# A mixture-of-experts layer behind an attention stage: where the routed stage is placed among the chunks of the shared expert, 38 ahead and 26 behind for 40 and 24

## The reference

```python
sg = xf @ shared_gate_w.T
su = xf @ shared_up_w.T
shared_out = jax.nn.silu(sg) * su @ shared_down_w.T      # 1024 hidden
topk_idx, w, _scores = _route(xf, router_w, correction_bias)   # 4 of 16 experts
...
h = jax.nn.silu(g) * u                                   # 128 hidden per expert
hw = h * combine.T[:, :, None]
routed = jnp.einsum('esh,ehc->sc', hw, down_w)
return (shared_out + routed).reshape(B, T, C)
```

## Time and profile before

| | us |
|---|---|
| median of 3 runs | 1007.53 (1004.88 to 1009.16) |
| profiled execution | 1004.85 |
| its span, first to last instruction | 1003.0 |
| granted TensorE clock, share of full | 0.999 |
| PE busy in the span | 985.6 (98%) |
| DVE, POOL, ACT busy | 660.1, 437.1, 380.6 |

### The profile page before, as it was taken

The page is one execution under the profiler, slowest core; times in us unless marked ns, Lnnn a source line. Parts: engine busy times, 40 slices in busy tenths (PEclk is TensorE's granted clock), DMA queues, the critical chain, the costliest instruction groups (busy, mean ns, idle before and its releaser), DMA issues.

```text
span 1003.0 us, 21036 instructions
## 1 busy us (share of the span) xinstructions
PE 985.6 (98%) x6750; PEld 601.2 (60%) x6750; DVE 660.1 (66%) x1534; ACT 380.6 (38%) x776; POOL 437.1 (44%) x508
## 2 busy tenths in 40 slices
PE   9999999999999999999999999999999999999997
PEld 7776744444444444446787777878778744344442
DVE  4977688874588898875455554555545436676767
ACT  3646454433544333223444444444444411111111
POOL 0726422131145222134545444454454167776774
PEclk9999999999999999999999999999999999999999
DMA  9736858878463611416999999999888578988776
GB/s 347 259 121 206 293 182 233 227 206 237 156 179 99 200 62 63 144 35 178 265 269 256 271 267 256 255 269 249 243 242 252 173 210 267 309 272 283 242 239 219
DMA packets 176636, 219.02 MB, mean 218 GB/s; under 512 B 101225, under 2 KB 112361, under 8 KB 175529
## 3 DMA queue, kind: packets, MB, share of 16 engines
q1 hardware_dynamic: 152792, 139.05, 46.6%
q0 software_dynamic: 23760, 78.79, 26.0%
HBM read 124.72 MB, written 70.27 MB: 194 GB/s over the span
## 4 chain that ended last, share of the span: by engine, by line
PE 87%; DVE 5%; issue 3%; DMA 2%; ACT 2%; another core or an unknown queue 0%; POOL 0%; DVEq 0%; SPq 0%; ACTq 0%; POOLq 0%
PE bank L1074 19%; PE bank L948 18%; PE bank L1137 11%; PE bank L964 9%; PE bank L1098 9%; PE bank L1149 5%; PE bank L1057 5%; PE bank L723 2%; PE bank L703 2%; PE bank L1088 2%; PE bank L800 1%; DMA arena<-in_dn_w 1%; PE bank L980 1%; PE bank L713 1%; PE bank L807 1%
## 5 line engine op out<-in xcount | busy, mean ns | idle before, releaser
L948 PE MATMUL bank<-arena 128*128 128x512 f16 x960 | 218.1, 379 | 0.2 <-ACT arena L1330 0.2
L1074 PE MATMUL bank<-arena 128*128 x1716 | 211.2, 273 | 1.0 <-DVE arena L1615 0.8
L1074 PEld LDWEIGHTS bank<-arena 128*128 128x128 f16 x1716 | 162.9, 98 | 26.9 <-issue 2.0
L2070 POOL DMA_INDIRECT arena<-xr_dram,arena x143 | 140.7, 984 | 57.7 <-issue 45.9
L2127 POOL DMA_INDIRECT arena<-y_dram,arena x128 | 134.4, 1050 | 70.9 <-issue 32.9
L948 PEld LDWEIGHTS bank<-arena 128*128 128x128 f16 x960 | 94.2, 99 | 108.2 <-ACT arena L1330 0.7
L1137 PE MATMUL bank<-arena 128*128 128x512 f16 x576 | 129.2, 379 | 1.6 <-issue 1.5
L1098 PE MATMUL bank<-arena 128*128 x429 | 115.4, 378 | 0.5 <-ACT arena L1408 0.5
L1345 ACT ACTIVATE arena<-arena 128x512 f16<-128x512 f32 x64 | 40.3, 629 | 197.8 <-DVE arena L1623 96.0
L1890 DVE SCALAR_TENSOR_TENSOR arena<-bank,arena 128x128 f32<-128x128 f32 x143 | 41.6, 291 | 107.6 <-ACT arena L1397 82.8
L1953 DVE SCALAR_TENSOR_TENSOR arena<-arena 128x512 f32<-128x512 f32 x128 | 95.1, 750 | 25.4 <-DMA arena<-y_dram,arena 16.9
(11 more groups left out here) (226 smaller groups left out, 1281.7 us busy)
## 6 DMA issues: line engine op xcount, KB each, us to landing
y_dram<-arena SPq DMA_DIRECT2D x143, 256.0 KB
arena<-in_x SPq DMA_DIRECT2D x8, 1024.0 KB, 12.4
xr_dram<-arena SPq DMA_DIRECT2D x16, 512.0 KB, 3.8
x_dram<-arena SPq DMA_DIRECT2D x8, 1024.0 KB, 5.6
arena<-in_gu_w SPq DMA_DIRECT2D x16, 512.0 KB, 3.6
out<-arena SPq DMA_DIRECT2D x32, 256.0 KB
arena<-x_dram SPq DMA_DIRECT2D x5, 1024.0 KB
arena<-x1s_dram SPq DMA_DIRECT2D x20, 256.0 KB
```

Of the source, the lines that this page charges most:

```text
L948: last = mm(bank[half][:, :], (gu_hi_s, gu_lo_s)[wp][:, c, at:at + H], xt[:, xv * KC + kc, :], start=(n == 0), stop=(n == 3 * KC - 1))
L1074: last = mm(gate_up_bank(s, s)[:, 0:2 * H], rows[:, xv * KC + kc, :], only((gu_hi_r, gu_lo_r)[wp], e, slice(kc * 2 * H, (kc + 1) * 2 * H)) ...
L2070: pool.indirect_dma_start(out=dst, out_offset=None, in_=xr_dram[:, :], in_offset=bass.IndirectOffsetOnAxis(ap=token_now[:, r:r + 1], axis= ...
```

## The change

The routed stage starts after 38 chunks, that is after six of block 4's eight (CUT = 4 is that block). Block 4's partial sum is added to `x1b` before the routed stage and stays there; its last two chunks open the closing stage, into fresh banks, and are added at chunk 40. So block 4 is a closing block with 4 own turns, 16 old tiles are left for the others, and block 4's sum is neither stored nor read back. `x1b` is not free for block 5, whose rows SP loads in the closing stage, and the half of `xtb_p` that block 6 needs is read until chunk 39, so its quarter turns move into the closing stage too. CONVERT, HOT, PARTS_AT, PACE and the tables of loads are given anew. The total of products is the same.

```diff
--- before.py
+++ after.py
@@ -56,8 +56,8 @@
...
-FIRST = 5
-SPLIT = E // (FIRST - WITH)
+AHEAD = 38
+CUT = AHEAD // SH
...
-CONVERT = {15: 1, **{g: 1 for g in range(17, 24)}, **{g: 1 for g in (25, 26, 28, 29, 31, 32, 35, 37)}}
+CONVERT = {15: 1, **{g: 1 for g in range(17, 24)}, **{g: 1 for g in (24, 26, 27, 29, 30, 32, 34, 36)}}
 PLACES = 22
-HOT = {26: (0, 3), 27: (3, 6), 28: (6, 9), 29: (9, 11), 30: (11, 14), 31: (14, 17), 32: (17, 19), 33: (19, 22), 34: (22, 25),
-       35: (25, 27), 36: (27, 30), 37: (30, 32)}
-
-LAST = range(FIRST * SH, S // BLK * SH)
-OLD = (6, 7, 7)
-OUT_AT, IN_AT, QUARTER_AT = (10, 16, 22, 28), (36, 42, 48, 54), (60, 68, 76, 84)
-OLD_IN = {-1: (0, 1), 0: (2, 3), 1: (4, 5), 2: (6, 7), 7: (8, 9), 9: (10, 11), 11: (12, 13), 12: (14, 15), 16: (16, 17), 18: (18, 19)}
-X1_IN = {4: (24, 25), 5: (26, 27), 13: (28, 29), 14: (30, 31)}
-TURN_IN = (3, 6, 8, 10)
-PARTS_AT = (0, 4, *(6,) * 6, 4, *(6,) * 4, 4, 6, 6, 4, *(6,) * 6, 4)
+HOT = {26: (0, 3), 27: (3, 6), 28: (6, 9), 29: (9, 13), 30: (13, 16), 31: (16, 19), 32: (19, 22), 33: (22, 26), 34: (26, 29), 35: (29, 32)}
+
+LAST = range(AHEAD, S // BLK * SH)
+OLD = (0, 5, 5, 6)
+OLD_IN = {0: (0, 1), 1: (2, 3), 4: (4, 5), 6: (6, 7), 10: (8, 9), 11: (10, 11), 18: (12, 13), 19: (14, 15)}
+X1_IN = {-1: (20, 21), 0: (22, 23), 7: (24, 25), 8: (26, 27), 15: (28, 29), 16: (30, 31)}
+TURN_IN = {6: (5, 6, 7, 9), 7: (12, 13, 14, 17)}
+PARTS_AT = (0, 6, 6, 4, 5, 6, 5, 4, 6, 6, 4, 6, 6, 4, 5, 6, 5, 4, 6, 6, 4, 6, 6, 4, 5, 3)
 RING = 4
-PACE = (20, 37)
+PACE = (15, 26)
...
@@ -608,7 +609,7 @@
             for n in range(4, E):
                 routed_weights(n, n % 2)
-                if n in (9, 13):
+                if n in (9, 15):
...
             sp.wait_ge(s_expert, 1)
             turn_fourth(0, 0)
-            sp.wait_ge(s_sd, FIRST * SH)
+            sp.wait_ge(s_sd, AHEAD)
             turn_fourth(1, 1)
             for s in range(BLOCKS):
                 y_out(s, s % 4)
                 if s % 4 == 3 and s + 8 < BLOCKS:
                     turn_fourth(s // 4 + 2, s // 4 % 2)
-                if s in OUT_AT:
-                    x1s_tile_out(FIRST - 1, OUT_AT.index(s))
-                if s in IN_AT:
-                    if s == IN_AT[0]:
-                        sp.wait_ge(s_x1sw, 16 * (FIRST - 1 + TB))
-                    x1_tile_in(FIRST, IN_AT.index(s))
-                if s in QUARTER_AT:
-                    quarter_turned_in(FIRST + 1, xtb_p[:, (FIRST + 1 - WITH) % 2, :, :], QUARTER_AT.index(s))
...
@@ -678,16 +664,19 @@
                     old_in(t // TB, t % TB)
                 for t in X1_IN.get(n, ()):
                     x1_late_in(t // TB, t % TB)
-                if n in TURN_IN:
-                    quarter_turned_in(NB - 1, xt_end, TURN_IN.index(n))
+                for k, moments in TURN_IN.items():
+                    if n in moments:
+                        if k < NB - 1:
+                            sp.wait_ge(s_su, SH * (k - 1))
+                        quarter_turned_in(k, turned_at(k), moments.index(n))
...
@@ -962,7 +951,7 @@
                         last = mm(bank[2 + t][:, :], s_hb[:, g % 2, hv, t * P:t * P + P], (dn_hi_s, dn_lo_s)[wp][:, c, :],
-                                  start=(c == 0 and n == 0), stop=(c == SH - 1 and n == 2))
+                                  start=(c == 0 and n == 0), stop=((c == SH - 1 or g == AHEAD - 1) and n == 2))
...
@@ -1638,7 +1626,7 @@
             def shared_sum(k, order=range(TB)):
 
-                dve.wait_ge(s_sd, SH * (k + 1))
+                dve.wait_ge(s_sd, min(SH * (k + 1), AHEAD))
...
@@ -1941,14 +1931,16 @@
-                    if m < FIRST * TB:
+                    if m < CUT * TB:
                         dve.wait_ge(s_old[m // TB], 16 * TB)
-                    elif k == FIRST:
-                        dve.wait_ge(s_x1i, 16 * (FIRST + TB))
+                    elif k == CUT:
+                        dve.wait_ge(s_x1s, TB * (CUT + 1))
...
@@ -1966,12 +1958,12 @@
             def sum_at(k):
-                dve.wait_ge(s_cmb, TOP_E * (of_block[k - FIRST][TB - 1] + 1))
+                dve.wait_ge(s_cmb, DONE_AT_CUT if k == CUT else TOP_E * (of_block[k - CUT][TB - 1] + 1))
...
@@ -1981,7 +1973,7 @@
                 ahead = 0 if c == 0 else 1
                 hidden_at(n, parts[:ahead])
-                if c == 0 and k > FIRST:
+                if c == 0:
                     sum_at(k - 1)
```

More of the change, by code:

```diff
@@ L229, in build @@
         ybuf = [view(o + 8 * KB * r, [TOP_E, D]) for r in range(RING)]
[L230 removed]
+        old = [view(o + 8 * KB * (RING + k), [TB, D]) for k in range(CUT)]
         xt_end = view(o + 88 * KB, [2 * KC, BLK], F16)
[L232 removed]
+        x1_end = {CUT: x1b, **{k: view(o + 8 * KB * (RING + k - 1), [TB, D]) for k in range(CUT + 1, NB)}}
         o4 = o3 + 12 * KB
@@ L989, in next_attention @@
                 attention(n, t, 6)
-            for g in range(FIRST * SH):
+            for g in range(AHEAD):
                 k, c = g // SH, g % SH
```

82 lines of the change are left out of this document (39 added, 43 removed).

## The result

| | before | after |
|---|---|---|
| median, us | 1008.35 (1004.88 to 1010.42, 4 runs) | 1026.38 (1014.47 to 1029.06, 4 runs) |
| ratio, 95% interval | | 1.0131 (1.0078 to 1.0184) |
| profiled execution; span | 1004.85; 1003.0 | 1029.06; 1027.2 |
| granted clock, share of full | 0.999 | 0.979 |

The account below looks back on a forecast made before the run. The prediction took PE (TensorE), busy 985.6 of 1003.0 us, as the bound; only its idle time could change. +4.0 + 2.1 - 2.3 = +3.8 us gave 1011.3 us on the median, range 1002 to 1018.

Parts of the forecast that it names:

- rival (a): Closing stage, chunk 48: block 6's last quarter turn arrives late and PE waits; 2 to 8 us, 1013 to 1019, chance 0.2.
- Term 1: Passage to the routed stage: POOL's last subtraction ends too late, so PE waits for the first gathers; +4.0 us.
- so no term for the clock: All stretches read: clock at full rate even through PE's idle pieces of 3 to 5 us, so nothing added.
- Term 2: One-hot comparisons squeezed into ten chunks leave DVE no slack, so PE waits in the shared chunks; +2.1 us.
- Term 3: Closing stage: 26 chunks for 128 combinations, fewer per chunk, so the stalls at its end shrink; -2.3 us.
- I keep 4.6 us: Closing stage, chunk 48: DVE stood idle there, so fewer combinations would not shorten that stall of 4.6 us.
- nearer 4: Closing stage: guessed landing time in us of one quarter turn alone, where a whole block took 10.2 us.
- any lateness of DVE over 1 us decides: Chunk 46: DVE late by over some 1 us makes block 6's last quarter late; DVE is at times 4 to 7 late.
- Rival (b): Closing stage: fewer gathers per chunk end all its stalls, -9.2 us for -2.3, so 1004.4 us; chance 0.2.

Follow-up runs that it names:

- e1: Changed kernel with block 6's quarter turns issued after turns 1, 2, 3, 4 instead of 5, 6, 7, 9; 1009.84 us, ratio 1.0022 on chip A.
- e3: Changed kernel with block 6's quarters after turns 1, 2, 3, 4 and the last conversion in chunk 35 instead of 36; 1007.44 us, ratio 0.9965 on chip A.
- e11: Kernel before, nothing edited, profiled on chip C; 1010.28 us, ratio 0.9998.
- e9: Kernel before with a 128x256 float16 product ahead of each of the first 16 narrow pairs; 1007.89 us, ratio 0.9971 on chip C.
- e14: Changed kernel with the same two edits as e3, run on chip E; 1004.28 us, ratio 1.0032.
- e8: As e3, but combinations ahead of chunk 48 packed as in the kernel before, six in each of chunks 42 to 47; 1008.96 us, ratio 1.0096 on chip B.

## Why the prediction was wrong, step by step

Between the profiled executions 24.2 us came for the forecast 3.8. What failed most in the sum are two terms put at nothing. Block 6's quarters had no term, only rival (a): 11.2 us of wait. The clock had none either: 3.0 us behind that wait, 2.6 us at the passage, and 10 us in the early stretch, which no change of the code brought.

- **Term 1, +4.0 us: the mechanism and its waits right, the price wrong.** POOL's subtraction came a chunk too late, its wait of 4 us was gone, and PE waited 3.45 and 1.40 us (3.7 and 0.9 forecast), for a gather that landed in 3.49 us (3.56). The step that failed is "so no term for the clock". It was drawn from idle pieces of 3 to 5 us with the clock at 1.00, but the 4.6 us at chunk 48 were several pieces with products between them, the longest 2.92 us; after, the clock fell behind these two waits, which made +4.0 into +7.0. e1 to e3 takes most of it back, 5.0 us by the lowest runs.
- **Term 2, +2.1 us: right.** 0.30, 0.63 and 0.92 us in chunks 28, 31 and 33, 1.85 in all, for 0.3, 0.6, 1.2 and 0.1 in chunks 30, 31, 33 and 35. A group of comparisons that meets the subtraction takes 3.8 us for 0.99, in every profile here. The Trainium skill (SBUF — State Buffer, SBUF: two separate sides) says that GpSimd and a VectorE instruction in a two-port mode, or with two inputs in SBUF, contend for a shared port pair, which the one that starts first gets for its whole instruction while "the other fully blocks". The trace of before agrees: a group that starts at 436.28 us, just ahead of the subtraction of 436.78 to 440.03, ends at 440.08.
- **Term 3, -2.3 us: mis-sized; all 9.2 us went.** "I keep 4.6 us" at chunk 48 was the step. I had read DVE's idle time there as something that comes with the chunk. It is one of the waits without a releaser, which come on some chips, and behind which the stall wanders (chunk 48 in one profile of before, 56 in e11). A single profile had given me a place for what has none.
- **Rival (a), 0.2, price 2 to 8 us: this was the case, at 11.2 us and 3.0 us of low clock.** The chain was the one described, quarter behind combination 40. Two sizes failed: a transfer "nearer 4" us took 13.36 under a DMA share of 0.88, and its issue was late, by DVE behind a gather of 9.23 us and by SP behind the third quarter. The earlier trace rows had also been misread: a load of x rows of 1 MB was issued 0.5 us before that block's quarters, and their own bytes moved in the second half of the 10.2 us (the last number of the last row is GB/s):

```profile
333.88 0.38 SPq L526 DMA_DIRECT2D arena<-x_dram  x1
334.36 6.65 SPq L512 DMA_TRANSPOSE arena<-xr_dram  x1
...
341.00:342.00 1.00, 1.00 (x6) 0.49 (x5) 0.48 (x1) 0.49 (x1) 1.00 (x1) 1.00 1.27 290
```

  The Trainium skill (DMA: Bandwidth & Descriptors, Latency and other measured facts) has DMA transposes, with a middle dimension that is not contiguous, at an effective 261 GB/s; an estimate from that is 1 us for a quarter of 256 KB. The 290 GB/s from 341 to 342 us are near that figure, so it is not the rate that failed here: 13.36 us are the time from issue to landing, with 4.46 us of issue in it and other transfers on the same engines. The chance was the other error: I had written that any lateness of DVE over 1 us decides, and had lateness of 4 to 7 us in the rows. That should have been the forecast.
- **Rival (b), 0.2: its outcome came as well, hidden beside (a).** e1 shows it alone on chip A: passage and one-hots paid, closing stage without a stall over 0.5 us, lowest run 0.5 us over that of before. Its reason, gathers that arrive just in time, is not shown: on chips B and E the kernel before has no such stalls to relieve. I had treated (a) and (b) as exclusive; they add.
- **Not in any term: the early clock**, 10 us in the profiled execution of after and none in that of before. It comes in some executions of both kernels and not in others, so one profile of each can differ by 10 us with no cause in the change. The sum on the profiled execution (1004.85, clock 0.999) took the lower bunch for the kernel.

## What to carry to other kernels

Before a transfer is moved behind a running stage, take its landing time from a row of that stage, not from a quiet one (10.2 us for four quarters behind one load, 13.4 for one here), look at what was issued just before it, and put it where the work that releases it can be late by as much. If a wait of PE opens, price the clock behind it too. Compare the lowest runs and the runs with a full clock apart, and take a second profile before a stall is given a place: two things here, a fall of up to 10 us and 9 us of stalls, came and went without any edit.

## What the runs showed that I had not expected

- PE's clock fell to half with PE never idle (after, 50 to 70 us), in a stretch of narrow products (128x2 and 128x128, float32). 15 of the 35 runs of before on chip A are in the slower bunch, at clocks of 0.985 to 0.992. With 16 products of 128x256 in float16 ahead of the first 16 pairs no profile had this fall; one between 95 and 140 us still came.
- Behind idle pieces of 3.40 (e9), 3.70 (e14), 3.97 (e11) and 4.07 us (e8) twelve down products took 5.28, 5.30, 5.18 and 4.37 us for 2.75; behind 2.92 us they took 2.75.
- One DMA_TRANSPOSE of a quarter held SP for 1.24 to 8.91 us, all in the closing stage of one profile (after).
- ACT, DVE and POOL have waits whose end nothing in the trace explains, 18 to 101 us in the closing stage, in all nine profiles of chips A, C and the first one and in none of the eight of B, D and E; at one place a silu came 5.0 us later than on E. That PE's signals are late there is my inference.
